# A two-layer FFN kernel: the first conditional net in three parts, most of its gate/up by Strassen's products

## The reference, cut to what matters

```python
def cond0(x, ids):            # 512 -> 1376 -> 512, adapters of rank 16 picked per sample
    gate = x @ W_gate.T + (x @ A_gate[ids].T) @ B_gate[ids].T * 0.5
    up   = x @ W_up.T   + (x @ A_up[ids].T)   @ B_up[ids].T   * 0.5
    act  = silu(gate) * up
    return act @ W_down.T + (act @ A_down[ids].T) @ B_down[ids].T * 0.5
def ffn0(x):                  # 512 -> 1792 -> 512, weights w * (su @ sv)
    return lin(silu(lin(x, gate)) * lin(x, up), down)
x = x + ffn0(cond0(x, ids0))
x = x + ffn1(cond1(x, ids1))  # cond1: one 512x512 linear with adapters; ffn1: int4 weights, 512 -> 1792 -> 512
```

## Time and profile before

| | |
|---|---|
| median of the runs | 620.11 us |
| span of the profiled execution | 618.3 us, with 8106 instructions |
| around the span (median less span) | 1.8 us |
| TensorE busy | 611.3 us (99%), 2958 matmuls |
| VectorE, ScalarE, POOL busy | 444.9, 313.2, 243.6 us |
| cond, gate/up a and b, down a and b | 6 to 210 us |
| ffn0, cond1, ffn1 | 210 to 618 us |

### The profile page before, as it was taken

One profiled execution on the slowest core, in us unless ns is written; L12 is line 12 of the kernel. 1 busy time (PEld: TensorE's weight loads), 2 busy tenths in 40 slices (PEclk: granted clock), 3 DMA queues, 4 the chain that ended last, 5 costly groups with the idle time before them and its releaser, 6 DMA issues.

```text
span 618.3 us, 8106 instructions
## 1 busy us (share of the span) xinstructions
PE 611.3 (99%) x2958; PEld 499.8 (81%) x2958; DVE 444.9 (72%) x544; ACT 313.2 (51%) x415; POOL 243.6 (39%) x194
## 2 busy tenths in 40 slices
PE   8999999999999999999999999999999999999997
PEld 6787888788778878788878888888788888888885
DVE  4585564644458999886247887645879998999987
ACT  5675615344354444452014444334657886478860
POOL 3670010000000006861034566530004889958896
PEclk9999999999999999999999999999999999999999
DMA  8750022101013111411211101152222121222203
GB/s 257 192 147 28 25 88 89 52 18 46 21 49 94 35 34 56 151 60 60 68 35 68 55 15 57 42 108 69 82 73 99 64 72 52 103 68 80 74 1 137
DMA packets 24826, 45.19 MB, mean 73 GB/s; under 512 B 10132, under 2 KB 12404, under 8 KB 24724
## 3 DMA queue, kind: packets, MB, share of 16 engines
q1 hardware_dynamic: 22484, 40.97, 21.3%
q0 software_dynamic: 2016, 3.19, 1.9%
q10 hardware_dynamic: 288, 0.52, 0.2%
HBM read 40.74 MB, written 2.10 MB: 69 GB/s over the span
## 4 chain that ended last, share of the span: by engine, by line
PE 98%; DMA 1%; SPq 0%; DVE 0%; ACT 0%; issue 0%
PE ps_down L2010 8%; PE ps_down L2011 7%; PE ps_down L2012 7%; PE ps_up L2010 4%; PE ps_up L2011 4%; PE ps_up L2012 4%; PE ps_gate L2142 3%; PE ps_gate L2199 3%; PE ps_gate L2198 3%; PE ps_up L2198 3%; PE ps_gate L2143 3%; PE ps_gate L2144 3%; PE ps_gate L2010 3%; PE ps_up L2199 3%; PE ps_m L2198 3%; PE ps_m L2199 3%
## 5 line engine op out<-in xcount | busy, mean ns | idle before, releaser
L876 POOL TENSOR_TENSOR act_lo<-up,act_hi 128x512 fp32r<-128x512 f32 x14 | 18.1, 1294 | 174.0 <-ACT act_hi L1176 174.0
L2010 PE MATMUL ps_down<-act_hi,w_hi 128*128 128x512 f32 x176 | 69.0, 392 | 0.0
L2011 PE MATMUL ps_down<-act_lo,w_hi 128*128 128x512 f32 x176 | 68.6, 390 | 0.0
L2012 PE MATMUL ps_down<-act_hi,w_lo 128*128 128x512 f32 x176 | 68.5, 389 | 0.0
L917 POOL TENSOR_TENSOR up_sum<-up_sum,up_more 128x1024 f32<-128x1024 f32 x14 | 33.7, 2406 | 61.9 <-DVE up_more L1551 61.9
L1416 DVE TENSOR_TENSOR w_lo<-w_raw,w_hi 128x512 fp32r<-128x512 f32 (+3 forms) x41 | 39.2, 955 | 13.3 <-ACT w_hi L990 9.3
L990 ACT ACTIVATE w_hi<-w_raw 128x1024 fp32r<-128x1024 f32 (+3 forms) x30 | 26.5, 884 | 43.6 <-PE ps_down L2012 17.9
L2012 PEld LDWEIGHTS ps_down<-act_hi,w_lo 128*128 128x128 f32 x176 | 33.0, 188 | 7.0
L1551 DVE SCALAR_TENSOR_TENSOR gate_sum<-ps_up,s_group,gate_sum 128x1024 f32<-128x1024 f32 x28 | 35.8, 1280 | 3.8 <-PE ps_up L2199 3.7
L2010 PEld LDWEIGHTS ps_down<-act_hi,w_hi 128*128 128x128 f32 x176 | 33.1, 188 | 6.6
L2011 PEld LDWEIGHTS ps_down<-act_lo,w_hi 128*128 128x128 f32 x176 | 33.1, 188 | 6.5
(11 more groups left out here) (321 smaller groups left out, 1799.5 us busy)
## 6 DMA issues: line engine op xcount, KB each, us to landing
w_int<-in_ffn_gu SPq DMA_DIRECT2D x14, 512.0 KB, 3.5
w_raw<-in_cond_gu SPq DMA_DIRECT2D x9, 512.0 KB, 5.0
w_raw<-in_ffn_gu SPq DMA_DIRECT2D x9, 512.0 KB, 3.5
w_raw<-in_ffn_dn SPq DMA_DIRECT2D x8, 448.0 KB, 3.2
w_int<-in_ffn_dn SPq DMA_DIRECT2D x8, 448.0 KB, 3.2
xp<-in_x SPq DMA_DIRECT2D x8, 256.0 KB, 5.3
w_raw_third<-in_ffn_gu SPq DMA_DIRECT2D x4, 512.0 KB, 3.5
xp<-in_x SPq DMA_DIRECT2D x1, 2048.0 KB, 9.9
```

The costliest lines, as they stand in the source:

```text
L2010: nc.tensor.matmul(ps[0:m, :], w_hi[0:r, s, cols], rhs_hi(k, r), start=start and n == 0, stop=False)
L2011: nc.tensor.matmul(ps[0:m, :], w_hi[0:r, s, cols], rhs_lo(k, r), start=False, stop=False)
L2012: last = nc.tensor.matmul(ps[0:m, :], w_lo[0:r, s, cols], rhs_hi(k, r), start=False, stop=stop and n == len(ks) - 1)
```

## The change

The cond net goes in three parts, of 4, 3 and 4 tiles, each with its down phase. Tiles 0 and 1 stay plain; tiles 2 to 10 are made by the seven products. The adapter pairs are added into the banks where the results stand. The half-block sums of the weights are POOL's, and so is `act_lo` of most tiles; those of x (five sums for the cond net) are made once at the start by VectorE (3) and POOL (2). The weights of tile t + 1 are split during tile t, on two sets of buffers that are shared with the raw a_dn and the down weights. `b_rows` becomes a ring of 1024 columns, filled in five loads (one on POOL and SP together, one on POOL, three on SP), each piece split once and copied to the other half by a DMA (`copy_b`). POOL makes the mask before its first loads, and takes over the order of a_dn from VectorE; SP takes over the 16 loads of the factors from POOL. At the seam the block sums of the first FFN tile (`first_sums`, behind `cond_act_lo(10)`) and five of nine x sums go from VectorE to POOL; `lo_of_b` and `hi_of_b` of pieces 11 and 12 stand in tile 10. `t_down` runs in rounds of tiles (0,1), (2,3), (4,5), (6,7), (8,9) and (10). All buffers are placed anew. In the diff below the blocks are, in order: constants, SP, POOL, ScalarE, VectorE, TensorE.

```diff
+COND_TILES, COND_FIRST = (4, 3, 4), (0, 4, 7)
+FIRST_SEVEN = 2
+COND_STEPS = ("2", "3", "1", "4", "5", "g0", "6", "7", "u1")
+COND_SLOT = {2: 1, 3: 0, 4: 0, 5: 1, 6: 0, 7: 1, 8: 0, 9: 1, 10: 0}
+COND_BEFORE = {4: 3, 6: 4, 7: 5, 8: 6, 9: 7, 10: 8}
+T_ROUNDS = {2: (0, 1), 6: (4, 5), 8: (6, 7), 10: (8, 9)}
...
+B_LOADS = ((0, 4), (4, 7), (7, 9), (9, 11), (11, 13))
...
+            gu_a, down_a, gu_b, down_b, gu_c, down_c = phases[:6]
...
+            sp.wait_ge(pack_zero, 2)
+            for q in range(4):
+                for v in range(4):
+                    row = 32 * q + SR * v
+                    sp.dma_start(pack_raw[row:row + SR, :], d["factors"][min(q, 2)]).then_inc(pack_in, 16)
+            load(down_a, 0)
+            copy_b(3)
+            for o in range(1, HK):
+                load(down_a, o)
+            load(gu_b, 0)
+            copy_b(4)
+            load(gu_b, 1)
+            load(gu_b, 2)
+            copy_b(5)
+            load(down_b, 0)
+            copy_b(6)
+            load(down_b, 1)
+            sp.wait_ge(cond_seven, cond_step(6, "u1"))
+            for b in range(NB):
+                load_b(sp, b, 2, b_again_in[1])
+            load(down_b, 2)
+            load(down_b, 3)
+            load(gu_c, 0)
+            copy_b(7)
+            load(gu_c, 1)
+            sp.wait_ge(down_ready, down_b.d0 + CH * HK)
+            for b in range(NB):
+                load_b(sp, b, 3, b_again_in[2])
+            load(gu_c, 2)
+            copy_b(8)
+            load(gu_c, 3)
+            copy_b(9)
+            sp.wait_ge(cond_seven, cond_step(8, "u1"))
+            for b in range(NB):
+                load_b(sp, b, 4, b_again_in[3])
+            load(down_c, 0)
+            copy_b(10)
+            load(down_c, 1)
+            sp.wait_ge(cond_seven, cond_step(NKD - 1, "u1"))
+            sp.dma_start(w_raw_first[:, :], d["ffn0_gu"][0]).then_inc(first_raw_in, 16)
+            for o in range(2, HK):
+                load(down_c, o)
...
+            cond_sums(2)
             nc.gpsimd.iota(row_id[:, 0:1], [[0, 1]], base=0, channel_multiplier=1).then_inc(rows_ready, 1)
-            pool.wait_ge(start_lo, len(start))
             for b in range(A_DN_POOL):
                 load_a_dn(pool, b, a_dn_in[0])
+            nc.gpsimd.memset(pack_short[:, :, :].bitcast(F32), 0.0).then_inc(pack_zero, 1)
             pool.wait_ge(t_sums, CH)
+            pool.wait_ge(cond_x_summed, 3)
+            pool.wait_ge(cond_x_more, 2)
             nc.gpsimd.memset(pack_raw[:, :], 0.0).then_inc(pack_zero, 1)
-            nc.gpsimd.memset(pack_short[:, :, :].bitcast(F32), 0.0).then_inc(pack_zero, 1)
-            pool.wait_ge(pack_zero, 1)
...
+            pool.wait_ge(a_dn_in[0], 16 * 2 * A_DN_POOL)
+            pool.wait_ge(a_dn_in[1], 16 * 2 * (NB - A_DN_POOL))
+            for rows, k0, k1 in ((P, 0, NKD - 1), (F0_TAIL, NKD - 1, NKD)):
+                nc.gpsimd.tensor_copy(a_dn[0:rows, k0:k1, :, :],
+                                      a_dn_raw[0:rows, :, k0 * R:k1 * R].rearrange("p b (k r) -> p k b r", r=R)).then_inc(a_dn_ready, 1)
+            pool.wait_ge(a_dn_ready, 2)
+            cond_sums(3)
+            for t in range(3):
+                cond_act_lo(t)
+            pool.wait_ge(cond_seven, cond_step(2, "u1"))
             for b in range(NB):
-                load_b(pool, b, 1, b_again_in)
+                load_b(pool, b, 1, b_again_in[0])
+            cond_sums(4)
+            cond_sums(5)
+            cond_sums(6)
+            for t in range(4, 6):
+                cond_act_lo(t)
+            cond_sums(7)
+            cond_sums(8)
+            for t in range(9, NKD):
+                cond_sums(t)
+                cond_act_lo(t - 2)
+            for t in range(NKD - 2, NKD):
+                cond_act_lo(t)
...
+            for n, k in x_sums_pool:
+                first, second = (x_block(half, c, k) for half, c in x_terms[n])
+                pool.wait_ge(sum_done, named["cond down c"].d0 + x_tiles(n, k))
+                nc.gpsimd.tensor_tensor(x_part(x_total[n], k), first, second, ALU.subtract if n in (3, 4) else ALU.add).then_inc(x_early, 1)
...
+            def cond_tile(t):
+                cond_m2_to_sbuf(t)
+                if t == 2:
+                    for n in (6, 7):
+                        cond_x_high(n)
+                    for n in range(2):
+                        cond_act_hi(n)
+                elif not first_of_part(t):
+                    cond_act_hi(t - 1)
+                if not last_of_part(t):
+                    for piece in range(2):
+                        cond_piece(t + 1, piece)
+                else:
+                    tile_hi(down_phase(t), 0, 0)
+                if t == 3:
+                    hi_of_pack()
+                cond_silu_gate0(t)
+                if not last_of_part(t):
+                    cond_piece(t + 1, 2)
+                    cond_silu_gate1(t)
+                    hi_of_b(t + 1)
+                    return
+                if t == NKD - 1:
+                    for p in range(NKD, NBP):
+                        hi_of_b(p)
+                cond_silu_gate1(t)
+                cond_act_hi(t)
+            def cond_down(ph):
+                t = COND_FIRST[ph.part + 1]
+                tile_hi(ph, 0, 1)
+                tile_hi(ph, 1, 0)
+                hi_of_b(t)
+                cond_piece(t, 0)
+                tile_hi(ph, 1, 1)
+                for piece in (1, 2):
+                    cond_piece(t, piece)
...
+            def cond_tile(t):
+                m = tile_rows(t)
+                bank_a, bank_b, bank_c = (bank[0:m, :] for bank in seven_banks[COND_SLOT[t]])
+                m2, d, e, (up, gate) = cond_m2[0:m, :], cond_d[0:m, :], cond_e[0:m, :], cond_out[t % 2]
+                count, inside = cond_count(t), not last_of_part(t)
+                if t == 2:
+                    for n in range(2):
+                        for c in range(CH):
+                            plain_product(n, c)
+                    cond_piece(2, 2)
+                elif not first_of_part(t):
+                    cond_products(t - 1)
+                if t == 3:
+                    cond_piece(3, 2)
+                    lo_of_b(3)
+                dve.wait_ge(cond_m2_copied, count)
+                dve.wait_ge(cond_seven, cond_step(t, "3"))
+                nc.vector.tensor_tensor(d, bank_b, m2, ALU.subtract).then_inc(cond_diff, 1)
+                if t == 2:
+                    cond_x_low(6)
+                elif inside:
+                    cond_piece(t + 1, 0)
+                dve.wait_ge(cond_diff, count)
+                dve.wait_ge(cond_seven, cond_step(t, "1"))
+                nc.vector.tensor_tensor(e, bank_a, d, ALU.add).then_inc(cond_part, 1)
+                if t == 2:
+                    cond_x_low(7)
+                elif inside:
+                    cond_piece(t + 1, 1)
+                else:
+                    tile_lo(down_phase(t), 0, 0)
+                dve.wait_ge(cond_part, count)
+                dve.wait_ge(cond_seven, cond_step(t, "4"))
+                nc.vector.tensor_tensor(e, e, bank_c, ALU.add).then_inc(cond_both, 1)
+                if t == 3:
+                    pack_rows()
+                dve.wait_ge(cond_both, count)
+                dve.wait_ge(cond_seven, cond_step(t, "5"))
+                nc.vector.tensor_tensor(e, e, bank_b, ALU.subtract).then_inc(cond_rest, 1)
+                if t == 2:
+                    cond_piece(3, 0)
+                if t == NKD - 1:
+                    for p in range(NKD, NBP):
+                        lo_of_b(p)
+                if t > 3:
+                    dve.wait_ge(act_ready, CH * (t - 1))
+                    dve.wait_ge(t_read, t - 1)
+                dve.wait_ge(cond_seven, cond_step(t, "6"))
+                nc.vector.tensor_tensor(gate[0:m, :], bank_a, d, ALU.add).then_inc(cond_gate1, 1)
+                if t == 2:
+                    cond_piece(3, 1)
+                elif inside:
+                    cond_piece(t + 1, 2)
+                dve.wait_ge(cond_rest, count)
+                dve.wait_ge(cond_seven, cond_step(t, "7"))
+                nc.vector.tensor_tensor(up[0:m, :], bank_c, e, ALU.add).then_inc(cond_up0, 1)
+                if inside and t > 2:
+                    lo_of_b(t + 1)
+                if not inside:
+                    cond_products(t)
+                    if t < NKD - 1:
+                        cond_act_lo(t)
...
+            def cond_down(ph):
+                t = COND_FIRST[ph.part + 1]
+                tile_lo(ph, 0, 1)
+                if ph.part == 0:
+                    pack_long_factors()
+                cond_evict(ph, 0)
+                if ph.part == 0:
+                    pack_short_factors()
+                tile_lo(ph, 1, 0)
+                cond_evict(ph, 1)
+                lo_of_b(t)
+                cond_piece(t, 0)
+                tile_lo(ph, 1, 1)
+                cond_evict(ph, 2)
+                for piece in (1, 2):
```

(26 more changed lines are left out.)

823 lines of the change are left out of this document (474 added, 349 removed).

## The result

The changed kernel takes 640.4 us (median of four runs, 638.5 to 642.5), the kernel before 620.3 beside it: a ratio of 1.032, with a 95% interval of 1.030 to 1.035. It is slower by 20 us, where I had forecast 621.6 and a range up to 628. Its profiled span is 636.6 us.

The account below looks back on a forecast made before the run. TensorE, busy 99% of the span, was taken to bound the kernel by matmul count times pace. Terms -12.3 + 0.5 + 1.0 + 1.6 + 6.6 + 1.2 + 2.9 = +1.5 us gave 621.6 us, range 611 to 628.

Parts of the forecast that it names:

- two starts of a down phase: Where down phases begin: TensorE waits 0.2 us at each of two starts for late work.
- 54 matmuls: Tiles 2 to 10 go from 48 to 42 matmuls each, taking 12.3 us off TensorE.
- two more rounds of t_down: Sums over A_down come in six rounds instead of four, at 0.25 us a round: +0.5 us.
- start to tile 3: Waits for the a_dn copy in tile 2 (0.3) and tile 3's late adapter rows (0.7): +1.0 us.
- tiles 5 and 9: The chain to the next adapter product ends after TensorE wants it: 0.6 us late in each.
- second down phase: SP's eight b0 loads delay the weights: column 2 waits 4.7 us, column 3 another 1.9, in all +6.6.
- tile 10: Two b pieces split before the last gate sum make the products late for t_down: +1.2 us.
- seam: Between the two nets: less TensorE cover and a late copy of product 2, between 1.5 and 6, taken as +2.9 us.
- ten or so of VectorE's steps can take the extra 0.24: At the seam, POOL works 10 us where it rested, lengthening about ten VectorE steps by 0.24 us each.
- VectorE becomes the bound: Rival, chance 0.22: VectorE's two-SBUF-input steps alternate with POOL's at start, tiles 5 and 9, second down phase, seam: 628.5 us.
- the clock falls: Rival, chance 0.13: TensorE's clock falls in the second down phase's 4.7 us wait, +1.5 us per fall, 623.1 us.
- Covered but for the load: Rival, chance 0.27 with better: VectorE and ScalarE keep up, only SP's eight loads cost: 614.9 us, or 608.3 if hidden.

Follow-up runs that it names:

- cut run: Changed kernel with GpSimd's additions in the first net and at the seam cut to 8 columns, readers taking other values: 620.3 us, ratio 1.001.

## Why the prediction was wrong

Step by step, in its own order. The cut run is the changed kernel nearly without meetings (and with GpSimd's results early), so it tells apart what I mis-sized from what I left out. The two starts of a down phase, 0.4 in the forecast, are not listed: they are part of the down phases here.

| term | forecast | after | cut run |
|---|---|---|---|
| 54 matmuls | -12.3 | 54 fewer | the same |
| two more rounds of t_down | +0.5 | +0.3 (5.60 us against 5.29) | the same |
| start to tile 3 | +1.0 | +4.7 to tile 2, +2.7 in 2 and 3 | +1.8 to tile 2, +0.9 in 3 |
| tiles 5 and 9 | +1.2 | +4.4 | +1.0 |
| second down phase | +6.6 | +6.9 | +6.3 |
| tile 10 | +1.2 | +1.4 | +1.4 |
| seam (last down phase and first FFN tile against 29.88 + 9.86 - 24 x 0.227 = 34.3, less tile 10's 1.4) | +2.9 | +9.5 | +1.6 |
| time | 621.6 | 640.4 | 620.3 |

- The matmuls, their pace and the rounds were right. So was tile 10's b split, and so was the largest single term, SyncE's eight loads: a wait in the third column of the second down phase, 4.05 us against 4.7. That the term came out right is in part luck: its addends (9.6 + 2.5 + 1.0) make 13.1 us and not 12.9, column 3 waited 0.2 us and not 1.9, and matmuls at half rate, which the term doesn't have, took 1.5.
- The step that failed is the price of a meeting of VectorE and GpSimd. It stood in "ten or so of VectorE's steps can take the extra 0.24" at the seam and in 0.6 a tile for tiles 5 and 9; the start had none. The 0.24 was the mean over met and unmet steps of the kernel before. What a meeting costs is not a mean but what is left of the other's instruction: 2.2 us beside an x sum of 3.2 us, 0.3 to 1.1 beside block sums. The row that showed this, VectorE's step lasting 1.37 us where 0.69 is its length alone, stood in the prediction; I named it and then went by the mean. VectorE lost 25.4 us in all, where I had 2.4 at the seam and at most 1 in each of two tiles.
- Without meetings the time comes out 1.3 us under the forecast, but not every term does: the start to tile 3 cost 2.7 us and not 1.0 even there, and the seam 1.6 and not 2.9, which evens out. It was a forecast of the kernel's order, for engines that don't touch each other.
- The rival "VectorE becomes the bound" had the mechanism and the places: start, tiles 5 and 9, seam. Its price of 1.5 us each for the tiles was low (2.2 each), the start's 2 were 4.7 and 2.7 more in tiles 2 and 3, and the seam's 6 were 9.5. Its largest term, 8 for the second down phase, was 6.9, and meetings have little part in it: with GpSimd's additions cut the phase is 0.6 us shorter. It deserved the likeliest place: the trace before had GpSimd's pace for two inputs, and the sum of both engines' such work in a tile, 10.1 us of 10.5, could have been made from it.
- The rival "the clock falls" was right in mechanism and near in price: 1.5 us forecast a fall, 1.5 where one was compared, 4.5 for the four of the changed kernel's profile. I gave it one place, the 4.7 us wait; it came there and in three more, two of them behind waits under 2 us. The Trainium skill's rule, page "TensorE: Matmul & The Clock Gate", section "What's actually happening", is that an idle array falls back. The trace agrees in these four places; the two waits of 1.91 us in the same profile were followed by no fall.
- "Covered but for the load" fell: its argument was that the FFN's Strassen tiles show no wait. What differs in those tiles, as the prediction had against it, is that their product reads PSUM; no run tried which difference counts.
- The page "SBUF — State Buffer" of the Trainium skill, section "Who interferes with whom", says that a VectorE instruction with two SBUF inputs and a GpSimd one that reads SBUF contend for a shared port pair, and that this pair is an exclusive lock. Here the trace agrees: at the start x_lo ended 1.1 us, about its own length, behind GpSimd's sum. I had weighed the rule as the late end of each bound; taken as the rule it is, it would have given the result's side.

## What to carry to other kernels

Before work goes to GpSimd to relieve VectorE, add up for one stage what both do with both inputs in SBUF; if the sum nears the stage's length, as here with 10.1 us of 10.5, expect the move to cost more than it takes away, however idle GpSimd looks, and reordering to move much of the loss to another step. Price a shared resource by its worst row, not by a mean over steps that mostly missed it. And where a wait moves when its named cause is taken away, look at what else is queued.

## What the runs showed of the hardware

- GpSimd writing alone did no harm: beside its memset of 2304 columns (32.53 to 34.58 us), a two-input step of VectorE kept its length, 1.23 us. GpSimd's and VectorE's rows, of the run in which the copy of product 2 was moved:

```profile
32.53 2.05 POOL L1001 MEMSET pack_raw<- 128x2304 f32 x1
34.51 2.51 POOL L1005 COPY a_dn<-a_dn_raw 128x1280 f32<-128x1280 f32 x2
```

```profile
32.53 1.23 DVE L1676 TENSOR_TENSOR cond_x_lo<-cond_x_total,cond_x_hi 128x1024 fp32r<-128x1024 f32 x1
33.78 3.08 DVE L1676 TENSOR_TENSOR b_rows<-b_raw,b_hi 32x1024 fp32r<-32x1024 f32 x1
```

- The second row of each shows that a copy, with one input, is enough. Its main part ran from 34.51 to 35.77 us and kept its length, and VectorE's step, whose row starts 0.72 us ahead of the copy's, ended 1.1 us behind that main part. In the changed kernel's profile the same step began 0.08 us earlier, 0.75 us ahead of the copy, and took 1.22 us; the next one paid 0.9 us instead, and tile 2 began 2.2 us earlier. So 1.9 us of this step hang on which engine gets through first, and the starts of the rows don't tell which it will be.
- A step on 32 partitions was hit as one on 128: the small t_rows steps doubled (3.35 us instead of 1.71).
- A wait of 1.9 us was followed by a fall of the clock in some executions and not in others; behind a fall the matmuls start 0.43 us apart instead of 0.227, four to twelve of them in the profiles here.
